# Context operand of a gated cross-attention kernel: block loads and VectorE 32x32 turns in place of TensorE transposes and ScalarE copies

## The chip, the cores and the metric

The kernel runs on one core of a Trainium2 chip. The metric is the device time of one execution in microseconds; before the change it was 326.13 us, the median of three runs (325.7 to 327.31). Profile times are microseconds from the start of the profiled span.

## What is computed

A gated block on x (4 batches, 512 tokens, 256 features) with a context of the same size. In short:

```python
x = x + tanh(g_xattn[0]) * xattn(layernorm(x), ctx, ctx, mask, W_q, b_q, ...)
x = x + tanh(g_ffn[0]) * ffn(layernorm(x), gate_w, w1, w2)
# xattn: q = query @ W_q.T + b_q, k and v alike from the context; 16 heads of 16;
#   local attention in windows of 64: each query sees its window and the one before it, causally
#   softmax, times v, then @ W_o.T + b_o
# ffn: top-1 of 16 experts by gate_logits, capacity 160 tokens an expert,
#   gelu(tokens @ w1) @ w2, weighted by the gate's softmax
```

All numbers are float32.

## The kernel before

The program is written out by hand for each engine: five instruction streams, one for each engine, joined by semaphores. There is no scheduler; the order in the code is the order on the engine.

**The head** prepares batch 0. SP loads x, the context and the rest; ScalarE's own DMA queue loads W_q and W_k. VectorE takes the statistics of x (`x_stats`) and normalizes it (`x_norm`), with a square root on GpSimd between them. TensorE turns W_q, W_k, the context and the normalized x by transposes against an identity (`wT_of`, `ctxT_of`, `xnT_of`), with filler matmuls between them (`keep_warm`). What TensorE writes in PSUM is copied to SBUF by ScalarE (`take_wT`, `take_xnT`) or, for the context of batch 0, by VectorE. Then come k and q (`k_of`, `q_of`), and the first scores.

**Four attention batches** follow. A batch has 16 units of work (a window of 64 queries and half of the heads). For each unit TensorE computes scores (`scores`, four units a call), VectorE adds the mask and finds the extreme (`low_of`), ScalarE takes the exponentials (`exp`, L697, four instructions a unit), VectorE the reciprocal of the sums (`r_total_of`), GpSimd scales (`norm`), TensorE turns the probabilities (`probsT_of`), VectorE and ScalarE copy them in turn (`take_probsT`), and TensorE multiplies by v (`attend`). In between lie the projections of the next batch and the router of the one before (`route`, `choose`, `rank_of`).

The context of batch b + 1 is prepared in batch b. SP's `load_ctx` brings it as 128 rows of 256 features, four times (`ctx_rows`). TensorE's `ctxT_of` (L1381) turns it in two calls of four transposes into the PSUM bank `ps_wide`, and ScalarE's `take_ctxT` (L681) copies each half of the features to `ctxT`, partitions by features, 512 tokens wide. Between the two calls TensorE waits for the first copy, since both use one bank. `ctxT[:, k]` holds feature k * 128 + p on partition p; k and v are products with the turned W_k and W_v, in the same order of features.

**The experts** come last, from 173.6 us on: 16 of them, on TensorE, with their weights streamed in by SP. Their rows are already loaded as blocks of 32 rows by quarters of the features (`load_rows`, L326) and turned by VectorE (`turn_rows`, L1263).

The lines that matter below: L306 `load_ctx`, L648 ScalarE's weight loads, L1123 and L681 the copies of the turned context, L1358 the transposes of weights, L1373 those of x, L1381 those of the context, L1352 the fillers, L1402 k, L1391 q, L1413 v, L1432 scores, L927 `low_of`, L1018 the router's maximum, L311 the shift of v.

## Time and profile before

| | us |
|---|---|
| median of 3 runs | 326.13 (325.7 to 327.31) |
| profiled execution | 324.84 |
| its span | 323.1 |
| TensorE busy | 300.2 (93%) |
| VectorE busy | 196.2 (61%) |
| ScalarE busy | 175.1 (54%) |
| GpSimd busy | 164.5 (51%) |

The span is what the profiler saw of the engines; 1.7 us of the execution lie around it. Busy shares of the whole span mix three stages: the head up to 18.6 us, the attention up to 160 and its tail up to 173.6, and the experts. The chain that ended last gives TensorE 58% of the span and ScalarE 26%. A wait is put down to the engine that came last. The clock that the throttle granted TensorE is given as a share of full speed.

### The profile page before, as it was taken

What the parts mean: (1) busy time and instruction counts of PE and PEld (TensorE: products, weight loads), DVE (VectorE), ACT (ScalarE), POOL (GpSimd) and SP (SyncE); (2) the same over time, 40 slices, a digit from 0 to 9 for tenths busy, and PEclk for the clock granted to TensorE, in tenths of its full rate; (3) what the DMA queues carried; (4) which work ended last, traced back from release to release, by engine and by line L of the source; (5) the groups of instructions that cost most, each with busy time, mean ns of one, the idle gap of its engine ahead of it and who ended that gap; (6) DMA issues with size and microseconds to landing.
All of it is one profiled execution on the core that took longest, in us unless ns stands there. A gap on an engine that the chain in (4) does not pass through costs nothing.

```text
span 323.1 us, 8432 instructions
## 1 busy us (share of the span) xinstructions
PE 300.2 (93%) x2760; PEld 245.6 (76%) x2760; DVE 196.2 (61%) x953; ACT 175.1 (54%) x662; POOL 164.5 (51%) x193
## 2 busy tenths in 40 slices
PE   7869879999999999999899899999999999999994
PEld 3438646887758866777778679898998989898974
DVE  2888898898989879899984223432415161515133
ACT  3379999999999999999743011111120202111110
POOL 6469647789769974979855022131313121121322
PEclk9997999999999999999999999999999999999999
DMA  7821199017512280230233589697989898998900
GB/s 219 281 90 25 40 380 330 10 26 242 184 67 92 62 298 3 100 79 19 83 122 149 123 235 370 179 377 200 372 246 353 270 333 267 294 324 247 367 22 13
DMA packets 48470, 60.54 MB, mean 187 GB/s; under 512 B 14712, under 2 KB 41360, under 8 KB 46384
## 3 DMA queue, kind: packets, MB, share of 16 engines
q1 hardware_dynamic: 45328, 53.29, 51.9%
q0 software_dynamic: 2560, 6.25, 5.3%
q10 hardware_dynamic: 544, 0.52, 0.5%
q8 instruction: 20, 0.33, 0.4%
q14 instruction: 18, 0.15, 0.2%
HBM read 44.60 MB, written 14.19 MB: 182 GB/s over the span
## 4 chain that ended last, share of the span: by engine, by line
PE 58%; ACT 26%; DVE 8%; issue 5%; DMA 1%; POOL 1%; SPq 0%; DVEq 0%; POOLq 0%; ACTq 0%
PE bank L1728 22%; ACT probs L697 18%; PE bank L1741 16%; PE bank L1766 5%; PE bank L1391 3%; ACT probsT L710 3%; DVE probs L927 3%; ACT q_par L671 2%; PE bank L1402 2%; PE bank L1504 2%; PE bank L1444 1%; DMA x_all<-in_x_dram 1%; PE bank L1466 1%; PE bank L1751 1%; PE bank L1413 1%
## 5 line engine op out<-in xcount | busy, mean ns | idle before, releaser
L697 ACT ACTIVATE probs<-probs,low 128x128 f32<-128x128 f32 x256 | 99.3, 405 | 2.2 <-DVE low L927 2.2
L518 POOL TENSOR_TENSOR probs<-probs,r_total 128x512 f32<-128x512 f32 x64 | 66.3, 1047 | 19.1 <-DVE r_total L936 18.7
L1728 PE MATMUL bank<-xdT,w 128*128 128x160 f32 x512 | 72.4, 299 | 2.1 <-issue 1.6
L1728 PEld LDWEIGHTS bank<-xdT,w 128*128 128x128 f32 x512 | 71.0, 190 | 4.0 <-issue 3.3
L927 DVE CUSTOM_DVE_ANT_0 probs<-bank,mask_now 128x128 f32<-128x128 f32 x256 | 57.2, 284 | 8.0 <-PE bank L1432 7.6
L697 ACT ACTIVATION_READ_ACCUMULATOR probs<-probs,low 128x1 f32 x256 | 52.5, 205 | 0.0
L857 ACT ACTIVATE w_raw<-bank 128x480 f32<-128x480 f32 (+1 forms) x24 | 12.6, 526 | 61.0 <-PE bank L1728 39.1
L622 POOL DMA_INDIRECT out_dram<-base,place x16 | 14.0, 876 | 59.9 <-DVE base L1294 38.4
L631 POOL DMA_INDIRECT out_dram<-base,place x16 | 15.7, 980 | 53.2 <-DVE place L1287 42.1
L857 ACT ACTIVATE x_all<-bank 128x480 f32<-128x480 f32 (+1 forms) x24 | 12.6, 526 | 53.8 <-PE bank L1728 35.2
L1444 PE MATMUL bank<-ident,probs 128*128 128x128 f32 x256 | 36.2, 278 | 2.2 <-DVE probsT L946 1.8
L1304 DVE SCALAR_TENSOR_TENSOR base<-bank,base 128x256 f32<-128x256 f32 x15 | 7.2, 483 | 49.7 <-PE bank L1741 49.6
L1444 PEld LDWEIGHTS bank<-ident,probs 128*128 128x128 f32 x256 | 29.2, 143 | 8.7 <-issue 5.8
L1294 DVE SCALAR_TENSOR_TENSOR base<-bank,base 32x256 f32<-32x256 f32 x64 | 30.5, 477 | 8.0 <-PE bank L1766 6.1
L1263 DVE STREAM_TRANSPOSE xdT<-q_blocks 128x320 f32<-128x320 f32 x16 | 8.2, 510 | 38.5 <-DMA q_blocks<-expert_queue 32.2
L1741 PE MATMUL bank<-w,w_raw 128*128 128x256 f32 x128 | 28.9, 379 | 0.0
L1741 PEld LDWEIGHTS bank<-w,w_raw 128*128 128x128 f32 x128 | 23.9, 190 | 2.9
L1741 PE MATMUL bank<-w,x_all 128*128 128x256 f32 x112 | 26.0, 386 | 0.0
L1741 PEld LDWEIGHTS bank<-w,x_all 128*128 128x128 f32 x112 | 20.7, 190 | 5.4 <-issue 2.9
L1432 PE MATMUL bank<-kT,q_par 32*128 32x128 f32 x512 | 18.8, 283 | 5.7 <-ACT q_par L671 3.4
L545 POOL DMA_INDIRECT expert_queue<-rows,slot x16 | 16.6, 1037 | 13.1 <-issue 5.8
L1432 PEld LDWEIGHTS bank<-kT,q_par 32*128 32x128 f32 x512 | 15.9, 186 | 9.5 <-issue 4.9
(142 smaller groups left out, 485.1 us busy)
## 6 DMA issues: line engine op xcount, KB each, us to landing
w<-in_L_ffn_w_dram SPq DMA_DIRECT2D x32, 1024.0 KB
expert_queue<-empty_row SPq DMA_DIRECT2D x1, 5140.0 KB, 19.0
q_blocks<-expert_queue SPq DMA_DIRECT2D x64, 40.0 KB
base<-expert_queue SPq DMA_DIRECT2D x16, 129.0 KB
ctx_rows<-in_ctx_dram SPq DMA_DIRECT2D x4, 512.0 KB, 9.6
out_dram<-rows SPq DMA_DIRECT2D x4, 512.0 KB, 6.3
x_all<-in_x_dram SPq DMA_DIRECT2D x3, 512.0 KB, 7.3
v_shift<-v SPq DMA_DIRECT2D x12, 128.0 KB, 2.3
```

The lines of the kernel that those rows point to most:

```text
L518: pool.tensor_tensor(probs[:, i % NP_], probs[:, i % NP_], r_total[:, i % NP_].unsqueeze(2).to_broadcast([P, PAIRS, 2 * WINDOW]), ALU.mult ...
L545: pool.indirect_dma_start(out=queue, out_offset=bass.IndirectOffsetOnAxis(ap=slot[n % 2][:, t:t + 1], axis=0), in_=rows[n % 2][:, t, :], i ...
L631: pool.indirect_dma_start(out=out_rows, out_offset=bass.IndirectOffsetOnAxis(ap=place[i][:, 0:1], axis=0), in_=base[i][:, 0, 0:D], in_offs ...
L697: last = act.activation(probs[:, i % NP_, j], probs[:, i % NP_, j], ACT.Exp, scale=-1.0, bias=low[:, i % NP_, j:j + 1], accum_out=total[:, ...
L857: act.activation(hidden[i][:, ms[0]:ms[-1] + 1, :], ps_hidden[m][:, 0:n].rearrange("p (m c) -> p m c", c=CAP), ACT.Gelu_apprx_tanh).then_i ...
L927: last = dve.tensor_tensor_reduce(probs[:, i % NP_, j], ps_scores[j][:, i % 4 * P:(i % 4 + 1) * P], mask_now[:, w % 2, w // 2], 1.0, 3.0e3 ...
L1294: dve.scalar_tensor_tensor(rest[:, 0:D], ps_rest[i % 2][j * REST:(j + 1) * REST, 0:D], rest[:, D:D + 1], rest[:, 0:D], ALU.mult, ALU.add). ...
L1432: last = pe.matmul(ps_scores[j][:, wi * P:(wi + 1) * P], q_par[rows_j, g, w].rearrange("p e q -> p (e q)"), kT[rows_j, g, w * WINDOW:w * W ...
L1444: last = pe.transpose(ps_probsT[i % 2][:, j * P:(j + 1) * P], probs[:, i % NP_, j], ident[:])
L1728: last = pe.matmul(ps_hidden[m][:, c * CAP:(c + 1) * CAP], w1_sb[i % 2][:, k, f * P:(f + 1) * P], xdT[i % 2][:, k], start=(k == 0), stop=( ...
L1741: last = pe.matmul(ps_y[:, 0:D], hidden[i % 2][:, k, 0:P], w2_sb[i % 2][:, k], start=(k == 0), stop=(k == KF - 1))
L1766: last = pe.matmul(ps_rest[i % 2][j * REST:(j + 1) * REST, 0:D], hidden[i % 2][:, k, P:CAP], w2_sb[i % 2][:, k], start=(step == 0), stop=( ...
```

## The change

Each context batch is loaded as four transfers of 32 partitions. Transfer j takes quarter j of the features (64 of them, 256 bytes) of every row, and puts row s * 32 + r on partition j * 32 + r, block s. VectorE's 32x32 transposes turn these blocks straight into `ctxT`: two instructions of 128x512 a batch (`turn_ctx`). Partition p of `ctxT[:, k]` now holds feature 2 * p + k, so the transposes of W_k and W_v read their columns with a step of two. TensorE's `ctxT_of` and ScalarE's `take_ctxT` are gone, and TensorE no longer needs `ps_wide` for the context. In the head the four loads of batch 0 move from SP's queue to ScalarE's, between W_q and W_k, and TensorE has nine fillers in a row where it had three, eight transposes, three.

```diff
             def load_ctx(n):
-                if n > 0:
-                    sp.wait_ge(ctxT_ready, value(n - 1, 2, 2))
-                sp.dma_start(ctx_rows[:], ctx_in[n].rearrange("(t p) d -> p t d", p=P)).then_inc(ctx_in_s, 16)
+                sp.wait_ge(ctxT_turned, value(n - 1, 2, 2))
+                for j in range(P // BLOCK):
+                    sp.dma_start(ctx_blocks[j * BLOCK:(j + 1) * BLOCK],
+                                 ctx_in[n, :, j * KD * BLOCK:(j + 1) * KD * BLOCK].rearrange("(s r) c -> r s c", r=BLOCK)
+                                 ).then_inc(ctx_in_s, 16)
...
             load_x(0, T // 2, T, x_in_late)
-            load_ctx(0)
...
             load_w(0, W_q)
+            for j in range(P // BLOCK):
+                act.dma_start(ctx_blocks[j * BLOCK:(j + 1) * BLOCK],
+                              ctx_in[0, :, j * KD * BLOCK:(j + 1) * KD * BLOCK].rearrange("(s r) c -> r s c", r=BLOCK)
+                              ).then_inc(ctx_in_s, 16)
             load_w(1, W_k)
...
                 exp(b, 8)
-                take_ctxT(b + 1, 0, ps_wide)
                 exp(b, 9)
-                take_ctxT(b + 1, 1, ps_wide)
...
+            def turn_ctx(n, half):
+                if not 0 <= n < B:
+                    return
+                dve.wait_ge(ctx_in_s, 16 * (P // BLOCK) * (n + 1))
+                if n > 0:
+
+                    dve.wait_ge(v_ready, value(n - 1, 2, 2))
+                blocks = slice(half * (S // BLOCK // 2), (half + 1) * (S // BLOCK // 2))
+                dve.transpose(ctxT[:, :, half * (S // 2):(half + 1) * (S // 2)].rearrange("p k (s r) -> p s k r", r=BLOCK),
+                              ctx_blocks[:, blocks].rearrange("p s (r k) -> p s k r", k=KD)).then_inc(ctxT_turned, 1)
...
                 for k in range(KD):
                     for d in range(KD):
-                        last = pe.transpose(ps[:, k * D + d * P:k * D + (d + 1) * P],
-                                            w_raw[:, i, d, k * P:(k + 1) * P], ident[:])
+                        cols = w_raw[:, i, d, k * P:(k + 1) * P]
+                        if i in (1, 2):
+
+                            cols = w_raw[:, i, d].rearrange("p (m k) -> p k m", k=KD)[:, k]
+                        last = pe.transpose(ps[:, k * D + d * P:k * D + (d + 1) * P], cols, ident[:])
...
                 v_of(b, 1, ps_misc)
+                probsT_of(b, 4)
+                probsT_of(b, 5)
+                pe.wait_ge(v_taken, value(b, 2, 2))
+                xnT_of(b + 1, 1, ps_misc)
+                scores(b, 3)
                 if first:
                     pe.wait_ge(wT_taken[3], 1)
                 else:
                     pe.wait_ge(x1nT_taken, value(b - 1, 2, 1))
-                ctxT_of(b + 1, 0, ps_wide)
-                probsT_of(b, 4)
-                probsT_of(b, 5)
-                pe.wait_ge(ctxT_taken, value(b + 1, 2, 1))
-                ctxT_of(b + 1, 1, ps_wide)
-                pe.wait_ge(v_taken, value(b, 2, 2))
-                xnT_of(b + 1, 1, ps_misc)
-                scores(b, 3)
-                pe.wait_ge(ctxT_taken, value(b + 1, 2, 2))
                 attend(b, 0)
```

What stands on the engines, at three places. First ScalarE's stream at the start of the program, which is also its DMA queue. Before:

```order
L648 DMA w_raw<-in_L_xattn_W_q_dram 128x2x256
L648 DMA w_raw<-in_L_xattn_W_k_dram 128x2x256
L655 ACT_TABLE_LOAD
L655 ACTIVATE wT<-bank 128x512 x2
L661 ACTIVATE xnT<-bank 128x512 x2
```

And in the changed kernel:

```order
L649 DMA w_raw<-in_L_xattn_W_q_dram 128x2x256
L653 DMA ctx_blocks<-in_ctx_dram 32x16x64 x4
L649 DMA w_raw<-in_L_xattn_W_k_dram 128x2x256
L660 ACT_TABLE_LOAD
L660 ACTIVATE wT<-bank 128x512 x2
L666 ACTIVATE xnT<-bank 128x512 x2
```

Four loads of 32x16x64 now stand ahead of W_k.

Second, TensorE's stream from the first filler to k and q of batch 0. `idle_rows` are the fillers, `w_raw` with `ident` the transposes of W_q and then W_k, `xn` those of x. Before:

```order
L1352 MATMUL bank<-idle_rows 128x512 x7
L1358 MATMUL bank<-ident,w_raw 128x128 x4
L1352 MATMUL bank<-idle_rows 128x512 x2
L1358 MATMUL bank<-ident,w_raw 128x128 x4
L1352 MATMUL bank<-idle_rows 128x512 x3
L1381 MATMUL bank<-ident,ctx_rows 128x128 x8
L1352 MATMUL bank<-idle_rows 128x512 x3
L1373 MATMUL bank<-ident,xn 128x128 x8
L1352 MATMUL bank<-idle_rows 128x512 x2
L1402 MATMUL bank<-ctxT,wT 128x512 x2
```

In the changed kernel:

```order
L1359 MATMUL bank<-idle_rows 128x512 x7
L1369 MATMUL bank<-ident,w_raw 128x128 x4
L1359 MATMUL bank<-idle_rows 128x512 x2
L1369 MATMUL bank<-ident,w_raw 128x128 x4
L1359 MATMUL bank<-idle_rows 128x512 x9
L1383 MATMUL bank<-ident,xn 128x128 x8
L1359 MATMUL bank<-idle_rows 128x512 x2
L1404 MATMUL bank<-ctxT,wT 128x512 x2
```

The context's eight transposes are gone; the transposes of x still stand behind those of W_k, with nine fillers between.

Third, VectorE's stream in batch 0, from the copy of the turned probabilities of unit 4 to the next one. Before:

```order
L946 COPY probsT<-bank4 128x512
...
L957 TENSOR_SCALAR attT<-bank6,parity_mask 128x256
L959 SCALAR_TENSOR_TENSOR attT<-bank6,parity_mask,attT 128x256
L876 BN_STATS stats<-x_all 128x6 x4
L880 BN_AGGR mean_var<-stats 128x2 x4
L890 TENSOR_SCALAR xn<-x_all,mean_var,rstd 128x256 x4
L936 RECIPROCAL r_total<-total 128x4
L946 COPY probsT<-bank4 128x512
L936 RECIPROCAL r_total<-total 128x4
```

In the changed kernel:

```order
L952 COPY probsT<-bank4 128x512
L897 STREAM_TRANSPOSE ctxT<-ctx_blocks 128x8x2x32
...
L963 TENSOR_SCALAR attT<-bank6,parity_mask 128x256
L965 SCALAR_TENSOR_TENSOR attT<-bank6,parity_mask,attT 128x256
L871 BN_STATS stats<-x_all 128x6 x4
L875 BN_AGGR mean_var<-stats 128x2 x4
L885 TENSOR_SCALAR xn<-x_all,mean_var,rstd 128x256 x4
L942 RECIPROCAL r_total<-total 128x4
L952 COPY probsT<-bank4 128x512
L897 STREAM_TRANSPOSE ctxT<-ctx_blocks 128x8x2x32
```

One turn stands behind the copy of unit 4, ahead of `low_of` for units 12 and 13, the other behind the copy of unit 6, ahead of `low_of` for unit 14 and the router's steps.

## Rows read from the trace of the kernel before

**Rows 1.** Busy time by stretch: stretch and its length; then busy us (instructions) of PE, PEld, DVE, ACT, POOL.

```profile
18.60:55.50 36.90, 30.66 (x306) 22.25 (x305) 33.49 (x200) 35.86 (x158) 25.65 (x25) 0.95 0.49 163
55.50:92.50 37.00, 35.69 (x414) 27.52 (x413) 33.38 (x192) 36.45 (x156) 30.14 (x31) 1.00 0.35 108
92.50:130.00 37.50, 36.62 (x417) 27.91 (x416) 32.83 (x200) 36.21 (x150) 30.86 (x31) 1.00 0.36 115
173.60:323.10 149.50, 142.49 (x1040) 126.25 (x1040) 47.68 (x128) 25.51 (x49) 33.47 (x36) 1.00 0.78 252
```

**Rows 2.** Chain that ended last, in the head: start, length, engine and line.

```profile
8.26 1.39 DVE xn L890 x4
...
9.70 1.09 PE bank L1373 x8
10.79 0.43 PE bank L1352 x2
11.22 1.73 PE bank L1402 x4
...
18.60 3.19 ACT probs L697 x16
```

**Rows 3.** The same chain, in the first two attention batches.

```profile
35.95 0.45 PE bank L1381 x4
...
36.42 0.05 ACT ctxT L681
36.47 0.45 issue
...
38.55 0.48 ACT ctxT L681
...
81.34 0.24 DVE top L1018
```

**Rows 4.** Instructions that write one tile: count, ns least/median/most, first and last start.

```profile
L681 ACT ACTIVATE ctxT<-bank x6: 582/590/600, 36.4 to 110.8; 128x512 f32<-128x512 f32 x6
...
L1263 DVE STREAM_TRANSPOSE xdT<-q_blocks x16: 473/512/515, 172.1 to 294.7; 128x320 f32<-128x320 f32 x16
```

**Rows 5.** Waits of VectorE from 18.6 to 130 us: total, times, longest.

```profile
DVE probs L927 <- PE bank L1432: 4.4, 6, 1.1
...
DVE top L1018 <- PE bank L1504: 1.4, 2, 1.1
```

**Rows 6.** Timeline: start, length, engine, line, operation; ACTq and SPq issue transfers.

```profile
1.33 0.49 ACTq L648 DMA_DIRECT2D w_raw<-in_L_xattn_W_k_dram  x1
...
1.37 3.17 PE L1352 MATMUL bank<-idle_rows 128*128 128x512 bf16 x7 [1.37 <-POOL idle_rows L435]
...
5.17 0.59 PE L1352 MATMUL bank<-idle_rows 128*128 128x512 bf16 x2
...
6.00 0.66 PE L1358 MATMUL bank<-ident,w_raw 128*128 128x128 f32 x4 [0.23 <-DMA w_raw<-in_L_xattn_W_k_dram]
...
39.73 6.92 SPq L306 DMA_DIRECT2D ctx_rows<-in_ctx_dram  x1
65.70 0.47 SPq L311 DMA_DIRECT2D v_shift<-v  x1
...
140.63 1.98 SPq L326 DMA_DIRECT2D q_blocks<-expert_queue  x4
```

**Rows 7.** DMA queues at 3 to 5 us, then 142 to 146: packets, MB, share.

```profile
q10 hardware_dynamic: 400, 0.39, 55.9%
q1 hardware_dynamic: 390, 0.37, 53.1%
...
q1 hardware_dynamic: 666, 0.15, 22.3%
```

**Rows 8.** TensorE's gap (timeline), then the stretch (columns of rows 1, then clock).

```profile
23.75 1.17 PE L1432 MATMUL bank<-kT,q_par 32*128 32x128 f32 x32 [2.69 <-ACT q_par L671]
...
25.40:28.80 3.40, 3.40 (x11) 2.70 (x10) 3.40 (x35) 3.40 (x19) 3.32 (x5) 0.51 0.00 0
```

More of the change, by code:

```diff
@@ L112, in flamingo_kernel @@
         x_all = sb("x_all", [P, B, T, D])
-        ctx_rows = sb("ctx_rows", [P, T, D])
+        ctx_blocks = sb("ctx_blocks", [P, S // BLOCK, KD * BLOCK])
         xn = sb("xn", [P, T, D])
@@ L208, in flamingo_kernel @@
         xnT_ready, xnT_taken = sem("xnT_ready"), sem("xnT_taken")
-        ctxT_ready, ctxT_taken = sem("ctxT_ready"), sem("ctxT_taken")
+        ctxT_turned = sem("ctxT_turned")
         q_ready, q_taken = sem("q_ready"), sem("q_taken")
@@ L673, in take_q @@
                 last.then_inc(q_taken, 1)
-            def take_ctxT(n, k, ps):
-                if not 0 <= n < B:
-                    return
-                act.wait_ge(ctxT_ready, value(n, 2, k + 1))
-                act.wait_ge(v_ready, value(n - 1, 2, 2))
-                act.activation(ctxT[:, k], ps[:], ACT.Copy).then_inc(ctxT_taken, 1)
             def take_k(n, g, ps):
@@ L1116, in _ @@
             x_stats(0)
+            turn_ctx(0, 0)
             x_norm(0)
+            turn_ctx(0, 1)
             dve.wait_ge(const_step, 3)
@@ L1120, in _ @@
                               ).then_inc(parity_ready, 1)
-            for k in range(KD):
-                dve.wait_ge(ctxT_ready, k + 1)
-                dve.tensor_copy(ctxT[:, k], bank[k][:]).then_inc(ctxT_taken, 1)
             dve.wait_ge(parity_ready, 1)
@@ L1169, in _ @@
                 take_probsT(b, 4)
+                turn_ctx(b + 1, 0)
                 low_of(b, 12)
@@ L1177, in _ @@
                 take_probsT(b, 6)
+                turn_ctx(b + 1, 1)
                 r_total_of(b, 11)
@@ L1374, in xnT_of @@
                 last.then_inc(xnT_ready, 1)
-            def ctxT_of(n, k, ps):
-                if not 0 <= n < B:
-                    return
-                pe.wait_ge(ctx_in_s, 16 * (n + 1))
-                for t in range(T):
-                    last = pe.transpose(ps[:, t * P:(t + 1) * P], ctx_rows[:, t, k * P:(k + 1) * P], ident[:])
-                last.then_inc(ctxT_ready, 1)
             def q_of(n, g, ps):
@@ L1397, in k_of @@
                     return
-                pe.wait_ge(ctxT_taken, value(n, 2, 2))
+                pe.wait_ge(ctxT_turned, value(n, 2, 2))
                 if n == 0 and g == 0:
@@ L1554, in _ @@
             wT_of(1, bank[5])
-            keep_warm(bank[3], 3)
-            for k in range(KD):
-                ctxT_of(0, k, bank[k])
-            keep_warm(bank[3], 3)
+            keep_warm(bank[3], 9)
             for k in range(KD):
```

## Prediction

> **What bounds the kernel now.** I read the stages first, from the view that gives each engine's busy time in a stretch [rows 1]. From 173.6 us to the end TensorE is busy for 142.5 of 149.5 us: the expert part, which the change does not touch. In the attention batches (18.6 to 130 us) ScalarE is busy 35.9 of 36.9, 36.5 of 37.0 and 36.2 of 37.5 us, TensorE 30.7, 35.7 and 36.6, VectorE 33.5, 33.4 and 32.8. So ScalarE has some 1 us of idle time in a batch, VectorE 3.4 to 4.7. The first 18.6 us are a chain of another kind: the x load, its statistics, the normalization, TensorE's transposes, k, q, scores. There each step waits for the one before, and any lateness goes to the end of the run in full, since the batch that follows has a bound of its own and makes nothing up.
>
> Next the chain that ended last, in the head [rows 2]: VectorE normalizes x from 8.26, TensorE turns it from 9.70, two filler matmuls take 0.43, k starts at 11.22. Then the same chain in the batches [rows 3]: it passes through ScalarE's copies of the turned context (0.48 us each is what one adds), through a stall of 0.45 us while ScalarE waits for the first of these, through TensorE's transposes (0.45 us for four), and in the second batch it leaves ScalarE for TensorE and then VectorE (81.34, the router's maximum).
>
> **What goes, in batches 0 to 2.** ScalarE loses six copies of 590 ns [rows 4]. They overlap their neighbours, so on the chain they are 0.48 each: 0.96 a batch, 2.9 us in all, and batch 0's stall of 0.45 too, 3.4 us at most. TensorE loses 24 transposes at 0.45 us per four, 2.7 us, in front of the score matmuls for which VectorE waits 4.4 us in these batches [rows 5]. That makes the score matmuls earlier by up to 0.9 us a batch, and it lies partly beside ScalarE's gain, so I do not add it.
>
> **What comes, in batches 0 to 2.** VectorE gets six turns of 128x512. The nearest row is the same instruction on 128x320: 512 ns [rows 4]. By size alone it would be 0.82; if part of the 512 is fixed, 0.7. I take 0.78, so 1.6 us a batch, 4.7 in all. The first one stands after the copy of unit 4's probabilities, just where VectorE now waits for the scores; that wait (up to 1.1 us [rows 5]) hides it. The second stands ahead of the router's steps, where VectorE waits 1.1 us at its longest for the logits [rows 5]; in the second batch what follows is a VectorE chain. There, turn and shorter wait nearly cancel: of 0.96 I keep 0.6. For the three batches: 1.2 + 0.6 + 0.7, **2.5 us gained**. Bounds: 3.4 (all of the copies and the stall) gained, and, if all six turns lie on the path, 4.7 less 3.4, so 1.3 lost. The SP queue issues four transfers for one, about 0.5 us each by the four-fold load of the same pattern, 1.98 us [rows 6]; the context of batch n+1 is asked for almost a batch ahead and what is queued behind it on SP (the shifts of v) comes over 15 us later (39.73 and 65.70 [rows 6]), so I cost that at nothing. Should that cover go, the shift, and so the first attention product, would be late by about 1.5 us.
>
> **The head.** For batch 0 the context load leaves SP's queue for ScalarE's, between W_q and W_k, as four loads with runs of 64 floats. Before, W_k was issued at 1.33 and TensorE could turn it at 6.00 [rows 6]. Two things now stand ahead of it: four issues (2 us of ScalarE's queue) and 2048 packets of 256 bytes. Price of a packet: from 3 to 5 us, 790 packets of 1 KB took 55.9 + 53.1% of 16 engines' 2 us, 34.9 us, so 44 ns each, and the engines are full; 256-byte packets took 22.3% of 16 x 4 us for 666, so 21.4 ns [rows 7]. So the context is 2048 x 21.4 / 16 = 2.74 us of all engines, against 512 x 44 / 16 = 1.41 before.
>
> The Trainium skill (DMA: Bandwidth & Descriptors, Specifications) says that transfers under 512 B do not reach line rate. The trace agrees in kind: 21.4 ns for a quarter of the bytes of a 44 ns packet is half the rate. By a price of a full 44 ns a packet the load would be 5.6 us and W_k 2.9 us later still; the row decides.
>
> When does W_k land? If the engines did nothing else in that time, at 6.0 + 2.74 less about 0.3 for the context packets that they carried before W_k so far: 8.4. If SP's queue (biases, mask, W_v, gates, x of batch 1) takes half of their time throughout, at 6.0 + 5.5 = 11.5. From 3 to 5 us the two queues did move equal numbers, 400 and 390 [rows 7], so half is not far-fetched; but SP's queue will not be full all the time. I take 10.0. TensorE's order is W_k's transposes (0.66 us [rows 6]), nine filler matmuls (0.43 for two [rows 2], so 1.93), then the transposes of x. So these start at 10.0 + 0.66 + 1.93 = 12.6 in place of 9.70: **2.9 us late**. VectorE's own new path is shorter: context at about 9.3, a turn (0.78), the normalization (1.39 [rows 2]), 11.5; the second turn ends at 12.3, before k can start.
>
> Then the clock. TensorE would stand idle from about 5.8 (the end of the fillers of 5.17 [rows 6]) to 10.0. The trace has one such gap: idle for 2.69 us up to 23.75, and from 25.4 to 28.8 the granted clock is 0.51, the lower level of 1.2 GHz [rows 8]. The gap in the head will be longer. 3.4 us at half speed on the chain is **1.7 us lost**; at either level the fillers have a price in the trace, 3.17 us for seven at the start [rows 6] against 0.43 for two. Everything behind (x's transposes, k, q) is TensorE's own chain, so nothing hides this. Head: 2.9 + 1.7 = 4.6 us. The strided reads of W_k and W_v in their transposes are eight instructions, at nothing. SP's other transfers at the start are issued 0.5 us sooner; none of them is what the chain waits for.
>
> **Sum.** The profiled execution took 324.84 us (span 323.1); the median is 1.29 above it, and I put the difference on the median. -2.5 + 4.6 = +2.1: 326.13 + 2.1 = **328.2 us**.
>
> **Rivals.**
> 1. The load is cheap (not slower): the engines serve ScalarE's queue so well that W_k lands at its bound, 8.4, the transposes of x start at 11.0, 1.3 late, and the gap of TensorE is too short to drop the clock. For it: the SP queue is thinned by the context itself, and x's second half comes sooner. Against: equal shares from 3 to 5 us. -2.5 + 1.3 = -1.2: 324.9; with the full 3.4 in the batches 324.0. The forecast turns to "not slower" from a W_k landed before 9.6 us without a drop of the clock (2.5 = W_k + 2.6 - 9.7).
> 2. Packet for packet: with one packet of SP's queue for each of the context's, a 21 ns packet waits for one of 44 or more. 2048 pairs would be 8.3 us if SP always had one; with many 4-byte ones among them I put W_k at 12.5. Head 5.4 + 1.7 = 7.1, sum +4.6: 330.7. The Trainium skill (DMA: Bandwidth & Descriptors, Queues, rings and completion order) has each engine go round robin between queue rows packet by packet; 400 and 390 agree with it, but since all these packets were of one size they don't tell it from equal time.
> 3. VectorE becomes the bound of the batches: it has 3.4 to 4.7 us idle a batch [rows 1], mostly waits that would have to move with TensorE. If the turns land on its path and eat the gain, the batches give 0: +4.6, 330.7.
>
> **Chances.** Forecast 0.48, rival 1 0.27, rival 2 0.15, rival 3 0.10. About 0.5% (1.6 us) is what a measurement of this kernel can tell from no change. Faster by more: half of rival 1 and a little of the forecast with a better batch part, 0.19. Within: the rest of rival 1 and the near edge of the forecast, 0.26. Slower: 0.55. The range takes in rival 1 and most of rival 2: 323.8 to 331.5.
>
> **What would show it.** The first transposes of W_k near 10 us and those of x near 12.6; a context turn of 0.7 to 0.8 us; half clock in the head; the first exponential near 23 in place of 18.60 [rows 2]; batches shorter by 0.6 to 1.2 us, with ScalarE still without gaps. A first exponential before 20 us makes the prediction wrong by the head; batches as long as before, with VectorE's waits gone, make it wrong by rival 3.

## The result, and the profile after

The changed kernel takes **336.03 us**, the median of four runs (335.06 to 336.33); the kernel before, in runs beside it, 325.91 (324.67 to 327.31). The ratio is 1.031 (95%: 1.027 to 1.035). The profiled execution took 336.33 us, its span is 334.6, 11.5 more than before.

The page of the changed kernel, its length and the shares of the chain that ended last:

```profile
span 334.6 us, 8379 instructions
...
PE 63%; DVE 14%; ACT 11%; DMA 5%; issue 5%; ACTq 1%; POOL 0%; DVEq 0%; POOLq 0%
```

ScalarE had 26% of that chain before and has 11% now: it did leave the chain, and the kernel is slower all the same. The stages, with the columns of [rows 1] (busy time of PE, PEld, DVE, ACT, POOL, then clock, DMA share, GB/s), cut at the first exponential, at the starts of the next batches and at the first expert product:

```profile
26.73:61.55 34.82, 26.30 (x277) 18.79 (x275) 29.95 (x176) 30.93 (x135) 22.09 (x20) 0.90 0.48 159
61.55:97.83 36.28, 35.01 (x408) 27.08 (x404) 33.92 (x192) 34.63 (x147) 29.61 (x30) 1.00 0.49 124
97.83:134.05 36.22, 34.27 (x402) 26.23 (x401) 33.29 (x194) 34.17 (x145) 29.70 (x29) 1.00 0.37 116
184.90:334.60 149.70, 142.77 (x1040) 126.35 (x1040) 47.79 (x128) 25.53 (x49) 33.47 (x36) 1.00 0.78 252
```

As marks I use the first exponential of ScalarE and the instruction that writes `mask_now`, once a batch on VectorE. Before they stand at 18.60, 50.13, 86.69 and 122.95 us, after at 26.73, 61.55, 97.83 and 134.05. So:

| part | before | after | difference |
|---|---|---|---|
| head, to the first exponential | 18.60 | 26.73 | +8.1 |
| batch 0, from there to the mark | 31.53 | 34.82 | +3.3 |
| batch 1 | 36.56 | 36.28 | -0.3 |
| batch 2 | 36.26 | 36.22 | 0.0 |
| the rest of the span | 200.15 | 200.55 | +0.4 |

**The head.** The chain that ended last (start, length, what), which answers to [rows 2]:

```profile
3.47 9.41 DMA w_raw<-in_L_xattn_W_k_dram
...
12.92 1.13 PE bank L1369 x4
14.05 3.84 PE bank L1359 x9
17.89 1.04 PE bank L1383 x8
18.93 0.43 PE bank L1359 x2
19.37 1.72 PE bank L1404 x4
...
26.73 3.19 ACT probs L694 x16
```

The timeline of the same stretch (start, length, engine; in brackets the idle time ahead and who ended it), answering to [rows 6]:

```profile
1.32 2.12 ACTq L653 DMA_DIRECT2D ctx_blocks<-in_ctx_dram  x4
...
3.47 3.21 ACTq L649 DMA_DIRECT2D w_raw<-in_L_xattn_W_k_dram  x1
...
12.25 0.71 DVE L897 STREAM_TRANSPOSE ctxT<-ctx_blocks 128x512 f32<-128x512 f32 x1 [5.58 <-DMA ctx_blocks<-in_ctx_dram]
...
12.92 1.13 PE L1369 MATMUL bank<-ident,w_raw 128*128 128x128 f32 x4 [7.20 <-DMA w_raw<-in_L_xattn_W_k_dram]
```

W_k could be turned at 12.92 in place of 6.00 [rows 6], 6.9 us later. What stood between W_k and x's transposes before (3.70 us, from 6.00 to 9.70) would be 0.66 + 1.93 at full clock, 1.1 shorter. But TensorE had been idle for 7.2 us, and the granted clock is the lower one, 1.2 GHz, through most of what follows. Two stretches at that level, with the columns above:

```profile
7.90:18.10 10.20, 5.18 (x15) 2.72 (x16) 5.52 (x19) 1.28 (x3) 3.19 (x5) 0.50 1.05 294
55.60:59.10 3.50, 3.50 (x11) 1.90 (x10) 1.21 (x12) 1.64 (x7) 3.42 (x5) 0.51 1.07 379
```

Four transposes of W_k take 1.13 (0.66 before), nine fillers 3.84: together 2.4 more than at full clock. 6.9 - 1.1 + 2.4 = 8.2, the head's 8.1.

**Batch 0.** VectorE's second turn, what stands ahead of it, and k of batch 1 on TensorE:

```profile
50.45 1.39 DVE L871 BATCH_NORM_STATS2 stats<-x_all 128x6 f32<-128x256 f32 x4
...
52.18 1.35 DVE L885 TENSOR_SCALAR xn<-x_all,mean_var,rstd 128x256 f32<-128x256 f32 x4
...
54.11 0.70 DVE L897 STREAM_TRANSPOSE ctxT<-ctx_blocks 128x512 f32<-128x512 f32 x1
...
54.96 3.07 PE L1404 MATMUL bank<-ctxT,wT 128*128 128x512 f32 x4 [3.44 <-DVE ctxT L897]
```

TensorE waits 3.44 us for the second turn. Before, the same k waited 1.54 us, for ScalarE's `q_par`. It started at 45.19, 26.6 us after the first exponential, and ran 1.98 us. Now it starts 28.2 us after it and runs 3.07, its end in the second half-clock stretch. 1.6 + 1.1 = 2.7 of the 3.3; the rest was not taken apart.

The turn itself, in all eight places (ns least/median/most):

```profile
L897 DVE STREAM_TRANSPOSE ctxT<-ctx_blocks x8: 690/699/712, 12.3 to 126.2; 128x512 f32<-128x512 f32 x8
```

And VectorE's waits in the batches (26.7 to 138 us: total, times, longest), which answer to [rows 5], 4.4 and 1.4 before:

```profile
DVE probs L933 <- PE bank L1434: 2.1, 6, 0.8
DVE top L1024 <- PE bank L1506: 0.8, 1, 0.8
```

### The profile page after: what moved, and what is told of

Same layout as the page of the kernel before. It is cut to its first block, busy times and chain, and to the rows that moved or that the text cites. A ratio compares the mean times of both kernels' runs of the same rounds, so it can differ in the third digit from the quotient of the medians.

```text
span 334.6 us, 8379 instructions
## 1 busy us (share of the span) xinstructions
PE 301.4 (90%) x2730; PEld 244.9 (73%) x2731; DVE 199.4 (60%) x959; ACT 172.8 (52%) x656; POOL 164.3 (49%) x193
## 4 chain that ended last, share of the span: by engine, by line
PE 63%; DVE 14%; ACT 11%; DMA 5%; issue 5%; ACTq 1%; POOL 0%; DVEq 0%; POOLq 0%
PE bank L1723 20%; PE bank L1736 15%; ACT probs L694 8%; DVE probs L933 5%; PE bank L1761 4%; PE bank L1434 4%; PE bank L1446 4%; PE bank L1404 3%; DMA w_raw<-in_L_xattn_W_k_dram 3%; DMA w<-in_L_ffn_w_dram 3%; PE bank L1468 2%; PE bank L1482 2%; PE bank L1393 2%; PE bank L1359 1%; DVE probsT L952 1%
## 5 line engine op out<-in xcount | busy, mean ns | idle before, releaser
L694 ACT ACTIVATION_READ_ACCUMULATOR probs<-probs,low 128x1 f32 x256 | 50.8, 199 | 0.0
L852 ACT ACTIVATE w_raw<-bank 128x480 f32<-128x480 f32 (+1 forms) x24 | 12.6, 526 | 61.0 <-PE bank L1723 40.5
L623 POOL DMA_INDIRECT out_dram<-base,place x16 | 14.0, 874 | 57.5 <-DVE base L1301 37.3
L852 ACT ACTIVATE x_all<-bank 128x480 f32<-128x480 f32 (+1 forms) x24 | 12.6, 526 | 54.0 <-PE bank L1723 49.4
L1270 DVE STREAM_TRANSPOSE xdT<-q_blocks 128x320 f32<-128x320 f32 x16 | 8.1, 509 | 34.6 <-DMA q_blocks<-expert_queue 26.6
L1434 PE MATMUL bank<-kT,q_par 32*128 32x128 f32 x512 | 19.7, 292 | 7.0 <-ACT q_par L676 3.4
L1434 PEld LDWEIGHTS bank<-kT,q_par 32*128 32x128 f32 x512 | 16.8, 194 | 10.9 <-issue 6.4
```

Of the source, the lines that this page charges most:

```text
L623: pool.indirect_dma_start(out=out_rows, out_offset=bass.IndirectOffsetOnAxis(ap=place[i][0:REST, 1:2], axis=0), in_=base[i][0:REST, 1, 0:D ...
L694: last = act.activation(probs[:, i % NP_, j], probs[:, i % NP_, j], ACT.Exp, scale=-1.0, bias=low[:, i % NP_, j:j + 1], accum_out=total[:, ...
L852: act.activation(hidden[i][:, ms[0]:ms[-1] + 1, :], ps_hidden[m][:, 0:n].rearrange("p (m c) -> p m c", c=CAP), ACT.Gelu_apprx_tanh).then_i ...
L1434: last = pe.matmul(ps_scores[j][:, wi * P:(wi + 1) * P], q_par[rows_j, g, w].rearrange("p e q -> p (e q)"), kT[rows_j, g, w * WINDOW:w * W ...
```

## The experiments

All start from the changed kernel unless said otherwise. The batches are cut at the marks above, from the profiled execution. The ratio is to the kernel before in runs beside it, whose medians were 325.43, 325.35 and 325.18 for the three groups of runs. Times from different groups are best compared by their ratios.

| kernel | us | ratio (95%) | first exp. | batch 0 | 1 | 2 |
|---|---|---|---|---|---|---|
| before | 325.91 | 1 | 18.60 | 31.53 | 36.56 | 36.26 |
| changed | 336.03 | 1.031 (1.027-1.035) | 26.73 | 34.82 | 36.28 | 36.22 |
| wk_first | 336.45 | 1.033 (1.026-1.041) | 26.52 | 34.40 | 36.29 | 36.13 |
| ctx_on_sp | 333.90 | 1.025 (1.018-1.032) | 23.89 | 34.42 | 36.30 | 36.27 |
| turn_early | 333.09 | 1.022 (1.014-1.029) | 26.26 | 31.04 | 36.91 | 36.26 |
| fillers_30 | 334.27 | 1.025 (1.018-1.032) | 24.10 | 35.42 | 36.27 | 36.25 |
| all_three | 325.65 | 1.0005 (0.998-1.003) | 19.59 | 30.93 | 37.07 | 36.22 |
| no_turns | 325.17 | 0.998 (0.996-1.000) | 19.03 | 31.38 | 36.68 | 36.22 |
| broadcasts_late | 336.74 | 1.033 (1.028-1.037) | 28.04 | 34.82 | 36.27 | 36.22 |
| rows_on_act | 326.58 | 1.004 (1.000-1.008) | 19.48 | 31.53 | 36.54 | 36.22 |
| sp_waits | 332.24 | 1.021 (1.020-1.023) | 23.38 | 34.51 | 36.26 | 36.22 |
| copies_twice | 328.83 | 1.011 (1.010-1.013) | 18.68 | 32.49 | 38.38 | 37.17 |
| turns_twice | 327.28 | 1.007 (1.005-1.008) | 19.21 | 32.70 | 37.68 | 36.23 |
| turn_before_norm | 331.04 | 1.018 (1.016-1.019) | 24.05 | 31.02 | 36.87 | 36.22 |

### The head: does W_k behind the context make it late?

**wk_first** puts W_k ahead of the context on ScalarE's queue.

```diff
             load_w(0, W_q)
+            load_w(1, W_k)
             for j in range(P // BLOCK):
...
-            load_w(1, W_k)
```

> The changed kernel with W_k's load ahead of the four context loads on ScalarE's queue; nothing else moved. Theory (two gates in the head: W_k in front of the transposes of x, and the context in front of the normalization on VectorE): W_k can be turned near 6 us as before; the context still lands near 12.5 us, since the same packets share the engines, so VectorE's first turn is at 12.5, the normalization ends at 14.7, x is turned at 14.8 instead of 17.7, and TensorE's idle gap (6.7 to 14.8) still drops the clock, so the first exponential is at about 24.5 (26.73 in the changed kernel, 18.60 before). Time about 334. Rival (W_k alone is the head's loss): the transposes of x near 10 us, the first exponential near 19, time about 328.

Measured 336.45, no change (334 was expected). The timeline of this kernel:

```profile
6.38 0.65 PE L1369 MATMUL bank<-ident,w_raw 128*128 128x128 f32 x4
...
13.22 0.71 DVE L897 STREAM_TRANSPOSE ctxT<-ctx_blocks 128x512 f32<-128x512 f32 x1 [6.16 <-DMA ctx_blocks<-in_ctx_dram]
...
15.26 1.97 PE L1383 MATMUL bank<-ident,xn 128*128 128x128 f32 x8 [6.28 <-DVE xn L885]
```

W_k is turned at 6.38 (6.00 before the change), and it is worth nothing: the context now lands at 13.22, VectorE's first turn waits for it ahead of the normalization, and TensorE waits 6.28 us for that, at half clock behind it. So the order on this queue decides only which of two operands is late.

**ctx_on_sp** gives batch 0's context back to SP's queue, behind x, still as 256-byte blocks.

```diff
             load_x(0, T // 2, T, x_in_late)
+            load_ctx(0)
...
             load_w(0, W_q)
-            for j in range(P // BLOCK):
-                act.dma_start(ctx_blocks[j * BLOCK:(j + 1) * BLOCK],
...
             load_w(1, W_k)
```

> The changed kernel with batch 0's four context loads back on SP's queue, right behind the two loads of x, ahead of the biases and the mask. Theory (sharing of the engines with SP's small and broadcast loads costs the time, not the 256-byte packets as such): 2048 packets of 18 to 21 ns are 2.3 to 2.7 us, the row load was 1.4, so the context lands 1 to 1.5 us later than the 7.58 of before, at 8.6 to 9.1; the first turn then delays the normalization to about 9.7, x is turned near 11.2, the first exponential near 20.2; time about 329.5 with batch 0's second loss (3.3 us) still in. Rival (the blocks are slow wherever they are issued): context after 11 us, first exponential after 22, time over 331.5.

Measured 333.9, 4.4 us more than was expected. The context landed at 9.24, 3.0 earlier. But what followed it is new. VectorE's normalization and GpSimd's work on the mask, in the timeline:

```profile
9.87 3.38 DVE L883 TENSOR_SCALAR xn<-x_all,mean_var,rstd 128x256 f32<-128x256 f32 x4
...
10.04 0.67 POOL L500 CAST key_valid<-mask_u 128x512 bf16<-128x512 uint8 x1 [1.49 <-DMA mask_u<-in_mask_BxS_bf_dram]
10.79 2.31 POOL L504 TENSOR_TENSOR mask_next<-key_valid,causal 128x512 bf16<-128x512 bf16 x2
```

The same four instructions took 1.39 us before [rows 2]. Here they run beside GpSimd's three instructions and take 3.38; in wk_first, behind GpSimd's, 1.34. The turn ahead of the normalization moved it into that stretch. The Trainium skill (GPSIMD Engine Reference, Key points) says that GpSimd shares its SBUF interfaces with VectorE, with contention for VectorE's two-port modes or two SBUF inputs; these rows agree, with a factor of 2.4. Which of the two cases the normalization is, no row tells.

**turn_before_norm** and **all_three** tell that apart. Both have ctx_on_sp and turn_early (below); all_three also normalizes x ahead of both turns:

```diff
-            turn_ctx(0, 0)
             x_norm(0)
+            turn_ctx(0, 0)
             turn_ctx(0, 1)
```

> The changed kernel with batch 0's context loads on SP's queue behind x, both head turns behind the normalization of x, and the second turn of each batch ahead of the statistics (as in turn_early). Theory (the head's loss is all from what the context and W_k kept waiting): the context lands near 9.2, the normalization runs from 8.3 to 9.7 as before, the turns fill 9.7 to 11.0, k starts near 11.2, the first exponential is at 18.6 to 18.9. Batches as in turn_early: batch 0 about 0.5 us shorter than before the change, batches 1 and 2 the same, so 325.0 against 325.4 of before: no difference. Rival (with the head repaired the batches give the 2.5 us that were forecast): 323.0.

> all_three with one head turn ahead of the normalization of x and one behind it, as the changed kernel has them. Theory (the context lands at 9.2, and the normalization then runs beside GpSimd's cast and mask products, which slows it from 1.38 to 3.38 us as in ctx_on_sp): the first exponential near 23.9, 4 to 5 us behind all_three, 330. Rival (only the late landing counts): 1.5 us behind all_three, 327.

Measured 325.65 and 331.04, both near what was expected: this one swap is worth 5.4 us (5.6 by the ratios). The timeline of all_three:

```profile
6.31 0.76 PE L1367 MATMUL bank<-ident,w_raw 128*128 128x128 f32 x4
...
8.57 1.38 DVE L883 TENSOR_SCALAR xn<-x_all,mean_var,rstd 128x256 f32<-128x256 f32 x4 [1.44 <-POOL rstd L480]
9.87 1.30 DVE L895 STREAM_TRANSPOSE ctxT<-ctx_blocks 128x512 f32<-128x512 f32 x2
...
10.01 1.09 PE L1381 MATMUL bank<-ident,xn 128*128 128x128 f32 x8 [1.00 <-DVE xn L883]
```

Normalized from 8.57, x is turned at 10.01 (9.70 before). In turn_before_norm the normalization starts at 10.04 and takes 3.38 us, so x is turned at 13.47; half clock follows (k is 2.53 us on the chain for 1.72). Of the 4.5 us between the first exponentials 1.5 is the later start and 2.0 the slower normalization; the 1.0 that is left I put down to the clock. Another 1.2 us lies behind batch 2 (201.5 us of span for 200.3); I did not look for its cause.

### The head: why does the load take so long?

**broadcasts_late** moves the mask and the broadcast gates and biases behind W_v and x of batch 1 on SP's queue, to see whether their packets hold the context up.

```diff
-            sp.dma_start(mask_u8[:], mask.partition_broadcast(P)).then_inc(mask_in, 16)
...
-            sp.dma_start(bias_o[:], b_o.partition_broadcast(P)).then_inc(small_in, 16)
             load_x(1, 0, T, x_in[1])
+            sp.dma_start(mask_u8[:], mask.partition_broadcast(P)).then_inc(mask_in, 16)
...
+            sp.dma_start(bias_o[:], b_o.partition_broadcast(P)).then_inc(small_in, 16)
```

> The changed kernel with SP's broadcast loads (the mask, the two gates, the two output biases, where all partitions read one row of memory) moved behind W_v and x of batch 1. Theory (from 6 to 10 us the context's packets move at a quarter of the rate that they had from 4.5 to 5.5, while the engines are not full, because the mask's 2 KB packets, which take 118 to 226 ns each, hold up each engine in turn): the context lands near 10 and W_k near 10.7, x is turned near 15.5, time 333.5 to 334.5. Rival (one packet for one packet, whatever SP's queue holds): W_v and x in place of the mask keep the context back as long, W_k lands after 12.3, time 336 or more.

Measured 336.74: that theory fell. The context landed at 13.02, later than the 12.25 of the changed kernel, so the mask and the other broadcasts alone are not what holds it up. The DMA queues (q10 is ScalarE's, q1 SP's: packets, MB, share of 16 engines), 5 to 13 us of this kernel, then 5 to 12 of the changed one:

```profile
q1 hardware_dynamic: 2012, 1.29, 59.5%
q10 hardware_dynamic: 1966, 0.67, 35.1%
```

```profile
q10 hardware_dynamic: 1945, 0.66, 44.3%
q1 hardware_dynamic: 1470, 0.77, 43.5%
```

Over these 8 us the two queues moved 1966 and 2012 packets, nearly one for one, though SP's are on the mean twice as large (38 ns each, 59.5% of 128 us over 2012, against 23). Shares of equal time would give ScalarE's queue 1.65 packets for one of SP's, and from its first packets at about 4.4 us the context would land at 4.4 + 2 x 2.74 = 9.9, not at 13. The Trainium skill (DMA: Bandwidth & Descriptors, Queues, rings and completion order) says that each engine goes round robin between queue rows at the granularity of a packet. The sum over this window agrees, but it does not show that rule; and the page counts some 9 to 17 descriptors to a packet, where a packet of the profile is here one run of 256 bytes or 1 KB, so the two need not be the same thing. In the changed kernel the counts are 1945 to 1470 and the times nearly equal, 44.3 and 43.5%. Within broadcasts_late the counts go from 370 to 240 (5 to 6 us) to 199 to 240 (9 to 10 us), and from 5 to 7 us the engines are busy little more than half of the time although the context is waiting. So the two queues hold each other up by more than equal time would, and by what rule stays open.

**sp_waits** makes SP wait for the context before it issues what stands behind x.

```diff
+            sp.wait_ge(ctx_in_s, 16 * (P // BLOCK))
             for i, b in enumerate((b_q, b_k)):
```

> The changed kernel with SP waiting, behind its two loads of x, until batch 0's context has landed; all its other loads at the start come after. Theory (each 256-byte packet of ScalarE's queue was paired with a packet of SP's queue): alone on the engines, 2048 packets of 18 to 21 ns take 2.3 to 2.7 us from about 4.4, the context lands near 7.5 and W_k near 8.2, so x is turned at 10.8 to 11.3 instead of 17.7 and the first exponential comes at about 21 (the mask now lands later, near 12). Rival (block loads are slow in themselves, by their descriptors or by the slowest engine): context after 10, W_k after 10.7. Time 329 to 332 under the theory.

Measured 332.24, at the upper end of what was expected. Alone from 5 to 7 us, ScalarE's queue moves

```profile
q10 hardware_dynamic: 1482, 0.37, 141.2%
```

that is 2 us x 16 / 1482 = 21.6 ns a packet, near the 21.4 of [rows 7]. (The 21.4 was the time that a packet took; here packets overlap, at 30 ns each, and 21.6 is the pace.) The context lands at 8.67 and W_k at 9.17, in place of 12.25 and 12.9. So of the 6.9 us by which W_k was late, 3.75 (12.92 less 9.17) is the sharing with what stood behind x on SP's queue, and 3.2 is left with that queue quiet, near the 2.74 that the context's packets take. The first exponential, expected at about 21, comes at 23.38, because the clock still falls, after a gap of 3.30 us:

```profile
9.17 1.13 PE L1370 MATMUL bank<-ident,w_raw 128*128 128x128 f32 x4 [3.30 <-DMA w_raw<-in_L_xattn_W_k_dram]
10.09 4.05 PE L1360 MATMUL bank<-idle_rows 128*128 128x512 bf16 x9
```

**rows_on_act** is the other half: the kernel before, with its own 512 packets of 1 KB, moved to ScalarE's queue between W_q and W_k.

```diff
             load_x(0, T // 2, T, x_in_late)
-            load_ctx(0)
...
             load_w(0, W_q)
+            act.dma_start(ctx_rows[:], ctx_in[0].rearrange("(t p) d -> p t d", p=P)).then_inc(ctx_in_s, 16)
             load_w(1, W_k)
```

> The kernel before with only batch 0's context load, still as rows of 1 KB, moved to ScalarE's queue between W_q and W_k. 512 packets instead of 2048. Theory (what delays W_k is the number of packets ahead of it, each paired with one of SP's): 32 packets an engine instead of 128, so W_k lands near 8.5 and the context near 7.7, x is turned at 11 to 11.5 instead of 9.7, time about 327. Rival (the queue as such is slow, whatever the packets): W_k after 11, time over 329.

Measured 326.58 (1.004, 1.000 to 1.008): W_k is turned at 7.98, 2.0 late, and 0.9 of it reaches the first exponential, at 19.48. So 512 packets in that place make W_k 2.0 us late, and 2048 packets, of a quarter of the size, 6.9.

**fillers_30** takes the clock out: 32 fillers in place of 2 ahead of W_k's transposes, so that TensorE has no gap.

```diff
-            keep_warm(bank[3], 2)
+            keep_warm(bank[3], 32)
             wT_of(1, bank[5])
```

> The changed kernel with 32 filler matmuls in place of 2 between the transposes of W_q and those of W_k, so that TensorE is busy from 5 us to about 11.5 while it waits for W_k. Theory (TensorE's idle gap of 7.2 us dropped its clock: nine fillers took 4.05 us in place of 1.9, the four transposes of W_k 1.13 in place of 0.66): W_k still lands at 12.9, then 0.7 + 1.9, x is turned near 15.6 instead of 17.7 and the first exponential comes near 24.6; time about 334. Rival (the clock drop is put there by the profile, or work in the gap does not hold the clock): the fillers behind W_k take 3.8 us again, time 336.

Measured 334.27. The stretch from 5 to 20 us, clock 1.00 (the last column but two), then the timeline:

```profile
5.00:20.00 15.00, 14.95 (x66) 8.02 (x67) 6.85 (x26) 4.25 (x6) 7.12 (x11) 1.00 1.02 252
```

```profile
12.85 0.63 PE L1369 MATMUL bank<-ident,w_raw 128*128 128x128 f32 x4
13.32 2.11 PE L1359 MATMUL bank<-idle_rows 128*128 128x512 bf16 x8
15.26 1.04 PE L1383 MATMUL bank<-ident,xn 128*128 128x128 f32 x8
```

W_k lands as late as in the changed kernel, and x is turned 2.6 us sooner (15.26 for 17.89); the first exponential comes 2.6 sooner. That is the clock's price in the head. Of these, 1.8 reached the end: in batch 0 the wait for the second turn was still there, and the half-clock stretch behind it came earlier and was longer (50.7 to 57.5 us at 0.51).

### Batch 0: the second turn

**turn_early** moves the second turn ahead of the statistics of x.

```diff
                 take_att(b, 0)
+                turn_ctx(b + 1, 1)
                 x_stats(b + 3)
...
-                turn_ctx(b + 1, 1)
```

> The changed kernel with the second turn of a batch moved from behind the copy of unit 6's probabilities to ahead of the statistics and the normalization of x, right behind the first attention copy. Theory (in batch 0 k of batch 1 waited 3.44 us for that turn, then ran at half clock, together the 3.3 us that batch 0 lost over the head's loss): the wait for the turn is gone, k of batch 1 waits for q's copy again as before (1.5 us), no drop of the clock there; time about 333 (336.0 less 3). Rival (batch 0 lost its time to VectorE's amount of work, not to the place of the turn): about 336, k still waits over 2 us.

Measured 333.09, 2.9 less than the changed kernel. Its timeline:

```profile
49.64 0.70 DVE L897 STREAM_TRANSPOSE ctxT<-ctx_blocks 128x512 f32<-128x512 f32 x1
...
52.24 1.98 PE L1404 MATMUL bank<-ctxT,wT 128*128 128x512 f32 x4 [1.54 <-ACT q_par L676]
```

k waits for `q_par` again, as long as before the change, and at full clock; batch 0 is 31.04, and batch 1 gives back 0.6 (36.91). The loss of batch 0 was the place of one instruction.

### The batches: is there anything to gain?

all_three removes every loss that was found, has ScalarE's copies and TensorE's transposes gone, and takes 325.65: the time of before, not 2.5 less. **no_turns** goes on from there and takes the turns and context loads of batches 1 to 3 away as well (so k and v of all batches come from batch 0's context).

```diff
-                if b < LAST:
-                    load_ctx(b + 1)
...
-                turn_ctx(b + 1, 0)
...
-                turn_ctx(b + 1, 1)
```

> As all_three, but the context loads and turns of batches 1 to 3 are left out, so that k and v of all batches are made from batch 0's context: it shows what ScalarE's six copies and TensorE's transposes cost where nothing takes their place. Theory (VectorE's six turns of 0.70 us take back the gain): 2.5 to 3.4 us under before, 322.0 to 323.0, batches 1 and 2 each about 1 us shorter than the 36.3 us of before. Rival (the batches are bound by a chain that the copies were not on): the same as all_three within 0.7 us.

Measured 325.17, 0.2% under before with an interval that reaches to equal (0.996 to 1.000), where my theory wanted 2.5 to 3.4 us. So VectorE's new work is not what ate the gain. Batches 0 and 1 together last 68.09 us before, 68.00 in all_three and 68.06 in no_turns; batch 2 is 36.1 to 36.3 in every kernel but the one that lengthens it. What the chain passes through in batch 2, by line, before and then in no_turns:

```profile
by line: ACT probs L697 35.5%; PE bank L1402 10.5%; PE bank L1391 10.3%; issue 8.4%; ACT probsT L710 6.7%; PE bank L1504 4.7%; DVE probs L927 3.9%; PE bank L1466 2.8%; ACT x1nT L718 2.7%; ACT xnT L661 2.7%; PE bank L1444 2.4%; ACT q_par L67
```

```profile
by line: DVE probs L929 11.6%; PE bank L1440 10.5%; PE bank L1387 9.7%; PE bank L1428 9.5%; PE bank L1462 8.4%; issue 6.9%; PE bank L1398 5.5%; PE bank L1476 5.4%; PE bank L1409 4.8%; PE bank L1500 4.7%; DVE marks L1025 3.3%; DVE probsT L94
```

Before, ScalarE's exponentials are a third of it (18.5 us of ScalarE in all, 11.7 of TensorE). In no_turns ScalarE is not on it at all: 21.7 us are TensorE's and 12.0 VectorE's, scores to `low_of` to turned probabilities to products. My reading at first was that two chains run through a batch, one by ScalarE and one by TensorE and VectorE, equally long. But in batch 2 the change took 1.0 us of busy time from ScalarE (35.1 to 34.1) and 0.8 from TensorE (35.0 to 34.2), and the batch did not move. The timelines show where the time goes. GpSimd's last two scalings of its long stretch, and VectorE's `top` and `marks` of the router, which work on what TensorE's router matmuls gave, before and then in no_turns:

```profile
117.16 2.03 POOL L518 TENSOR_TENSOR probs<-probs,r_total 128x512 f32<-128x512 f32 x2
118.16 0.23 DVE L1018 TENSOR_REDUCE top<-bank 128x4 f32<-128x64 f32 x1 [1.07 <-PE bank L1504]
118.68 0.60 DVE L1023 SCALAR_TENSOR_TENSOR marks<-lowered,countdown 128x64 f32<-128x64 f32 x1
```

```profile
117.52 2.03 POOL L519 TENSOR_TENSOR probs<-probs,r_total 128x512 f32<-128x512 f32 x2
117.93 0.23 DVE L1020 TENSOR_REDUCE top<-bank 128x4 f32<-128x64 f32 x1 [1.08 <-PE bank L1500]
118.45 1.19 DVE L1025 SCALAR_TENSOR_TENSOR marks<-lowered,countdown 128x64 f32<-128x64 f32 x1
```

Counted from the mark, `top` starts at 31.47 before and at 30.84 in no_turns: TensorE is 0.6 us ahead. Then `marks` takes 1.19 us in place of 0.60, and ends at 32.55, where it ended at 32.59 before. Both times that is within 0.1 us of the end of GpSimd's scalings (32.50 and 32.46). In copies_twice (below) `marks` starts after GpSimd has ended and takes 0.23. In wk_first it starts in time to take 0.22, and it is the next product, `scaled`, that takes 1.08 and ends at 32.59. So there was a gain of 0.6 us in batch 2, and it is lost at a VectorE instruction that is stretched beside GpSimd, as the normalization was in the head. GpSimd itself works from 5.2 to 32.5 us after the mark without a gap of 0.2 us, at the same times before, in the changed kernel, in all_three and in no_turns. That GpSimd's stretch holds batch 2 at its length is read from these rows; no run shortened it. Batches 0 and 1 were not taken apart like this.

Two more kernels add work, to ScalarE or to VectorE. **copies_twice** is the kernel before with each of ScalarE's six copies done twice, **turns_twice** is all_three with each of the six turns done twice, the added one going to space that nothing reads in those batches. Neither loads one engine alone: TensorE waits for the copies and for the turns, so what waits for them comes later too.

```diff
+                act.activation([b_[:].rearrange("p a c -> p (a c)") for b_ in base + at_slot][2 * (n - 1) + k][:, 0:S], ps[:], ACT.Copy)
                 act.activation(ctxT[:, k], ps[:], ACT.Copy).then_inc(ctxT_taken, 1)
```

```diff
+                if n > 0:
+                    dve.transpose([b_[:].rearrange("p a c -> p (a c)") for b_ in base + at_slot][2 * (n - 1) + half][:, 0:S].rearrange("p (k s r) -> p s k r", k=KD, r=BLOCK),
+                                  ctx_blocks[:, blocks].rearrange("p s (r k) -> p s k r", k=KD))
```

> The kernel before with each of ScalarE's six copies of the turned context done twice (the first into a tile that nobody reads): 2.9 us more on ScalarE in batches 0 to 2. Theory (ScalarE's chain and a chain of TensorE and VectorE are equally long, so taking work from ScalarE gives nothing, while adding to it costs): 1.5 to 3 us slower than before, 327 to 328.5. Rival (ScalarE was never on the bound): no difference, 325.4.

> all_three with each of VectorE's six turns in the batches done twice (the first into a tile that nobody reads): 4.2 us more on VectorE, 0.70 each. Theory (VectorE had 3 to 4 us of waits a batch, and the first six turns cost 0.2 us in all by all_three against no_turns, so VectorE's slack is nearly used up): 1 to 3 us slower than all_three, 326.5 to 328.5. Rival (the turns lie fully beside other work): no difference, 325.6.

Measured 328.83, +3.7 us to before (1.011, 1.010 to 1.013; expected 1.5 to 3), and 327.28, 1.6 us over all_three by the medians and 2.0 by the ratios, as expected. The six added copies lengthen the batches by 0.96, 1.82 and 0.91, in all 3.7: added, they cost some 0.6 us each on the mean; taken away, they give nothing. Of 4.2 us of added turns 1.6 to 2.0 come out: batches 0 and 1 are 2.4 longer, the first exponential came 0.4 earlier in this profile, and batch 2 (36.23) hides its two.

## Why the prediction was wrong

It had the sign, at 0.55, and the steps of the head (W_k late, TensorE idle, the clock lower), but not their sizes, and it had the batches wrong. The sign was forecast as a small difference, 4.6 lost less 2.5 gained; it came out because the head lost nearly twice as much and the batches gained nothing. The forecast was 2.1 us slower, with a range to 331.5; measured 336.03.

- **W_k's landing, forecast 10.0, is 12.9.** This is the step with the clearest error. The price of a packet was about right (a pace of 21.6 ns alone, and W_k 3.2 us late with SP's queue quiet, where I had 2.4). The share of SP's queue was not: I gave it 1.6 us, and sp_waits shows 3.75. I took that queue to have half of the engines' *time* at most, which gave 11.5 as the upper bound, and 12.9 lies beyond it. Rival 2, packet for packet, put W_k at 12.5; I gave it 0.15 because [rows 7] could not tell the two. It had the size; whether it had the rule stays open (broadcasts_late). W_k's own 256 packets stand on the same queue behind the context's, and I gave them no share of the delay.
- **x's transposes, forecast 12.6, at 17.9.** 2.9 of this is the landing, 2.4 the clock on W_k's transposes and the fillers.
- **The clock, forecast 1.7, is 2.4 to 2.6** (fillers_30). The step was right; the gap was 7.2 us in place of 4.2, and W_k's transposes and the nine fillers ran at the lower level.
- **VectorE's path in the head ("shorter") was not looked at for its neighbours.** In the changed kernel W_k covers it. When W_k is early (wk_first) the context is just as late, and with the context early (ctx_on_sp) the normalization runs into GpSimd's mask work.
- **The turn, forecast 0.78, is 0.70**, the lower of the two values that I had weighed (0.7 and 0.82).
- **The second turn, at a wait of VectorE.** Wrong step: I asked what VectorE waits for around it and not who waits for it. TensorE's k of the next batch does, and in batch 0 the statistics and normalization of x stand ahead of the turn. +3.3 us. That TensorE then fell to half clock a second time was no part of any case.
- **A gain of 2.5 in the batches: it is 0.** I read "the chain passes through ScalarE's copies" as "without them it is shorter by them". The view shows one chain, and not how close behind it another one is. In batch 2 TensorE does come 0.6 us sooner, and VectorE's `marks` then takes 0.6 longer beside GpSimd. I had not looked at GpSimd at all: [rows 1] gives it 30 of 37 us, which looks like room, but its idle time lies at the ends of the batch. Rival 3 had the size (0) with the wrong reason: without any turns it is 0 as well.
- **The queued loads of SP in the batches at nothing:** right, no wait for them shows.

In us: head +8.1 for +4.6; batches +3.0 for -2.5; the rest +0.4 for 0.

What the changed kernel loses to the one before is taken apart: ctx_on_sp and turn_early give back 2.1 and 2.9 us alone and 5.0 together (turn_before_norm), the order of normalization and turns 5.4 more, which is the whole 10.4 us to all_three. Two things stay open: by what rule the two DMA queues hold each other up, and whether less work on GpSimd would let the freed time of ScalarE and TensorE count; no run tried that. No version was faster than the kernel before by more than can be told.

## What to carry to other kernels

Before taking an instruction off the chain that ended last, look for what would hold the stretch without it. That need not be an engine with a high busy share: look for one that works through without a gap (GpSimd here, at 30 of 37 us), and for instructions of its neighbours that end when it ends. And ask of every moved instruction who waits for its result, not only what it may hide behind. A load cut into smaller packets can be held up beside another busy queue for longer than its bytes suggest, and whatever is queued behind it waits too, so the place of such a load matters as much as its size.

## What the hardware showed that I had not expected

- 2048 packets of 256 bytes landed at 8.67 us with the other queue quiet (sp_waits) and at 12.25 and 13.02 beside it. Over 8 us the two queues moved 1966 and 2012 packets (broadcasts_late), over 7 us 1945 and 1470 (the changed kernel).
- Four 128x256 float32 normalizations on VectorE take 1.34 to 1.39 us alone and 3.38 beside GpSimd's cast and products of the mask, in three kernels (ctx_on_sp, turn_before_norm, broadcasts_late).
- The product `marks` on VectorE, 128x64, takes 0.23 us with GpSimd idle (copies_twice) and 1.19 when it starts 1.1 us before GpSimd's scalings end (no_turns); it then ends 0.1 us after them.
- One DMA issue can hold ScalarE's stream for long: that of W_k took 3.21 us behind the context's 2048 packets, 0.49 before [rows 6]. Here ScalarE had nothing else to do.
- A gap of TensorE of 3.3 us (sp_waits) was followed by the lower clock, 0.53 from 8.8 to 15.6 us: four transposes took 1.13 for 0.65 us and nine fillers 4.05 for 2.11, 2.4 us on top of the gap.
